# The first slots stage of a three-part language tower: from two passes of four sequences to one staggered sequence

## The chip, the cores and the metric

The kernel runs on one core of one Trainium2 chip. The metric is device time in microseconds (us), the median of several runs. The kernel is written by hand for the core's engines: TensorE (PE; its weight loads are shown as PEld), VectorE (DVE), ScalarE (ACT), GpSimd (POOL) and SyncE (SP, which issues the large DMAs). Each engine works off its own queue in order and waits on semaphores.

## What is computed

Eight sequences of 256 tokens with 192 features go through a token mixer, an attention layer and a two-level mixture of experts. The change lies at the start of the third part. Here is what matters of it, in the reference's words (G is the group of 64 tokens, g a token in it; e, s are 8 x 16 = 128 slots; the input h is first normalised per token over its 192 features):

```
xn = _l2norm(x) * scale * gamma_in
xg = xn.reshape(b, G, g, d)
phi = _l2norm(slots1) * scale
logits1 = jnp.einsum('bGgd,esd->bGges', xg, phi)
disp1 = jax.nn.softmax(logits1, axis=2)
comb1 = jax.nn.softmax(logits1.reshape(b, G, g, E1 * S1), -1)
slots = jnp.einsum('bGgd,bGges->bGesd', xg, disp1)
yn = _l2norm(slots) * scale * gamma2[None, None, :, None, :]
means = yn.reshape(b, G, E1, m, ns, d).mean(axis=4)
```

The stage leaves three things behind for the later ones: `yn`, the transposed `comb1` (`comb_t`) and the transposed `means` (`means_t`).

## The kernel before

The kernel is a chain of stages: `fold_weights` (folds weight products, and normalises and transposes the slot vectors into `phi_t`), `token_mixer`, `attention`, `first_slots`, `second_slots`, `second_dispatch`, `experts`, `combine`. A stage ends for all engines together, so what follows waits for the engine that ends last. All numbers are float32 in the stage that is changed. A float32 matmul appears in the trace as two MATMUL records, a transpose as one.

`first_slots` (L1181) treats the eight sequences in two passes of WIDE = 4. A sequence is 256 tokens, in TPS = 2 tiles of 128, or GPS = 4 groups of 64. Each pass goes through the same steps, and each step is done for all four sequences before the next one begins, in the queue of each engine:

- VectorE: token statistics (L1361, L1367); ScalarE turns variances into factors with a Ln and an Exp (`root`, L1289 and L1292); VectorE centres and scales (L1376) and multiplies by `gamma_in` (L1383), which gives `x`.
- TensorE transposes `x` in four pieces of 96 features by 128 tokens (L1234); ScalarE copies them out of PSUM (L1297).
- TensorE makes the logits in both orientations, contracting 96 + 96 features: slots by tokens (L1242) and tokens by slots (L1246).
- VectorE takes the maxima of both (L1388, L1391); ScalarE takes the exponentials with their sums (dispatch L1304, combine L1308).
- VectorE divides the combine weights (L1398, L1400). TensorE transposes dispatch (L1253) and combine (L1259). ScalarE copies dispatch into zero-padded tiles `disp`, 64 rows at a time (L1317), and VectorE keeps combine (L1406).
- TensorE makes the slots, each group as a contraction over 128 rows of which 64 are zeros (L1267). ScalarE squares and sums them one by one (L1333, each waiting for the one before). VectorE forms the variance (L1423, L1429), ScalarE takes its root (L1322, L1325), VectorE scales the slots (L1415).
- TensorE averages four slots at a time (L1274), ScalarE copies the result (L1341), TensorE transposes it (L1280), VectorE keeps it (L1438). ScalarE also copies the scaled slots into `yn_all` (L1344), which is the last instruction of the stage.

PSUM has eight banks; sequence `s` of a pass owns banks 2s and 2s + 1. GpSimd only clears the padding of `disp` (L1460, L1461). SyncE issues the loads of the next weights at the start of the stage (L1466, L1473, L1474). The next stage starts with VectorE's copy at L1596.

The order of ScalarE's queue at the end of a pass is typical of how the order is written out by hand:

```
for s in range(WIDE):
    act.wait_ge(S["slots_made"], at(i, s))
    for gr in range(GPS):
        ...
    if s:
        root_slots(s - 1)
root_slots(WIDE - 1)
```

## Time and profile before

| what | value |
|---|---|
| median of 3 runs | 716.32 us (715.44 to 719.78) |
| the profiled execution | 714.86 us |
| its span, first to last instruction | 713.1 us |
| lies around the span | 1.8 us |
| mean granted TensorE clock | 0.875 of full speed |
| `first_slots` | 349 to 421 us of the span |
| busy over the whole span | PE 81%, DVE 55%, ACT 43%, POOL 9% |

Full speed is 2.4 GHz, and the clock is either at that level (1.00) or at 1.2 GHz (0.50); a value between is a mix of both over a stretch. A busy time is the union of an engine's instructions. Instructions overlap in their engine, so a row's mean duration can be longer than the distance between two starts: for the cost of a queue the distance counts, for a handover the end.

### The profile page before, as it was taken

The numbers are of one execution on the slowest core, as the hardware profiler recorded it, in microseconds if no ns is written. First come the engines' busy times: TensorE is split into PE (matmuls) and PEld (weight loads), VectorE is DVE, ScalarE is ACT, GpSimd is POOL, SyncE is SP. The second block draws the span as 40 slices with busy tenths as digits, with TensorE's granted clock in tenths as the row PEclk, the third lists the DMA queues.
The fourth block names the chain that finished last, engine by engine and source line by source line (L and its number), as shares of the span: only waits on it lengthen the run. The fifth ranks groups of instructions, "written<-read, shape, count | busy, mean of one in ns | idle before, by whom it ended". The sixth has DMA issues, their size and how long they took to land. (4 is left out here: it accounts for less than half of the span.)

```text
span 713.1 us, 12372 instructions
## 1 busy us (share of the span) xinstructions
PE 580.8 (81%) x4294; PEld 473.8 (66%) x4294; DVE 390.7 (55%) x972; ACT 303.6 (43%) x859; POOL 64.9 (9%) x82
## 2 busy tenths in 40 slices
PE   6497996468888998887486968788889999999945
PEld 5486796255666665664374835577778999999934
DVE  2128646577999999964456344455653333333315
ACT  1223333143667666553177856555553222222211
...
DMA packets 19652, 58.19 MB, mean 82 GB/s; under 512 B 2627, under 2 KB 9397, under 8 KB 19478
## 3 DMA queue, kind: packets, MB, share of 16 engines
...
q8 instruction: 27, 0.44, 0.3%
q14 instruction: 19, 0.16, 0.1%
...
## 5 line engine op out<-in xcount | busy, mean ns | idle before, releaser
L1896 DVE SCALAR_TENSOR_TENSOR ex_act_t<-banks,b_sb,ex_gelu 128x128 f32<-128x128 f32 x128 | 36.0, 344 | 95.4 <-ACT ex_gelu L1879 95.4
L1879 ACT ACTIVATE ex_gelu<-banks,b_sb 128x128 f32<-128x128 f32 x128 | 36.6, 369 | 100.7 <-PE banks L1853 100.7
L1848 PE MATMUL banks<-slots_t,w 128*128 128x128 f32 x512 | 62.5, 275 | 1.1 <-PEq L1608 1.1
L1848 PEld LDWEIGHTS banks<-slots_t,w 128*128 128x128 f32 x512 | 61.2, 192 | 1.5 <-issue 1.3
L1074 DVE TENSOR_REDUCE att_max<-banks 128x4 f32<-128x1024 f32 x48 | 58.6, 1220 | 3.3 <-PE banks L736 2.4
L924 ACT ACTIVATE att_prob<-banks 128x1024 f32<-128x1024 f32 x48 | 49.1, 1023 | 17.2 <-PE banks L759 17.2
L1866 PE MATMUL banks<-w,ex_act_t 128*128 128x192 f32 x256 | 50.2, 339 | 0.2 <-DVE ex_act_t L1896 0.2
L1866 PEld LDWEIGHTS banks<-w,ex_act_t 128*128 128x128 f32 x256 | 40.7, 189 | 4.3 <-DVE ex_act_t L1896 0.5
L1853 PE MATMUL banks<-slots_t,w 64*128 64x128 f32 x512 | 37.2, 285 | 0.0
L736 PE MATMUL banks<-k_t,q_t 96*128 96x256 bf16 x192 | 31.9, 292 | 4.2 <-DVE att_max L1074 4.1
L774 PE MATMUL banks<-att_prob,val 128*32 128x256 f32 x384 | 29.2, 427 | 7.0 <-ACT att_prob L924 6.8
...
L759 PE MATMUL banks<-q_t,k_t 104*128 104x256 bf16 x192 | 31.0, 286 | 4.0 <-ACT att_prob L924 3.0
L1853 PEld LDWEIGHTS banks<-slots_t,w 64*128 64x128 f32 x512 | 31.1, 187 | 3.9
L709 PE MATMUL banks<-ident_b,att_stack 128*96 128x128 bf16 x384 | 28.3, 231 | 5.2 <-DVE att_stack L1041 2.4
L679 PE MATMUL banks<-qkv_t_sb,xt 96*128 96x384 f32 (+1 forms) x64 | 29.1, 591 | 3.3 <-ACT xt L870 3.3
L709 PEld LDWEIGHTS banks<-ident_b,att_stack 128*96 128x96 bf16 x384 | 26.2, 132 | 7.4 <-DVE q_t L1045 3.5
L899 ACT COPY k_t<-banks 96x1024 bf16<-96x1024 bf16 x24 | 24.1, 1006 | 15.3 <-PE banks L709 15.3
L1166 POOL TENSOR_TENSOR att_qk<-att_qk,qk_weight 128x192 f32<-128x192 f32 x16 | 9.2, 599 | 211.5 <-DVE att_qk L1009 211.5
L1529 PE MATMUL banks<-w_slot,ss_mean_k 96*128 96x384 f32 x64 | 23.9, 523 | 3.5 <-DVE ss_mean_k L1596 2.4
L736 PEld LDWEIGHTS banks<-k_t,q_t 96*128 96x128 bf16 x192 | 16.3, 103 | 13.4 <-DVE att_max L1074 8.4
L759 PEld LDWEIGHTS banks<-q_t,k_t 104*128 104x128 bf16 x192 | 18.2, 101 | 9.8 <-ACT att_prob L924 4.5
...
## 6 DMA issues: line engine op xcount, KB each, us to landing
...
```

Of the source, the lines that this page charges most:

```text
L679: last = nc.tensor.matmul(g.ps[banks[1 + t]][:, 0:2 * DIM], x_t[s][0:k, c, t * P:(t + 1) * P], g.t["qkv_t"][0:k, c, 0:2 * DIM], start=(c = ...
L709: last = nc.tensor.transpose(bank[0:KS, h * SEQ + t * P:h * SEQ + (t + 1) * P], stack[:, row, :, :].rearrange("p a b -> p (a b)"), ident_b ...
L736: last = nc.tensor.matmul(g.ps[hh][:, t * SEQ:(t + 1) * SEQ], q_t[s][0:KS, h, t * P:(t + 1) * P], k_t[s][0:KS, h, :], start=True, stop=True)
L759: last = nc.tensor.matmul(g.ps[2 + hh][:, m * SEQ:(m + 1) * SEQ], k_t[s][:, h, m * P:(m + 1) * P], q_t[s][:, h, :], start=True, stop=True)
L774: last = nc.tensor.matmul(bank[32 * j:32 * j + 32, (q % 2) * SEQ:(q % 2 + 1) * SEQ], val[s][:, m, QH * q + j, :], prob[j // 2][:, j % 2, m ...
L924: nc.scalar.activation(prob[u][:, :, :, :].rearrange("p a b n -> p (a b n)"), flat(2, 4), ACT.Exp).then_inc(S["exped"], 1)
L1074: nc.vector.tensor_reduce(neg_max[:, 2 * u:2 * u + 2, :].rearrange("p a b -> p (a b)"), flat(0, 2).rearrange("p (g n) -> p g n", n=SEQ), A ...
L1848: nc.tensor.matmul(bank[:, j * P:(j + 1) * P], g.w1[e][:, first + j * P:first + (j + 1) * P], x[:, 0, :], start=(j == 0), stop=False, skip ...
L1853: last = nc.tensor.matmul(bank[:, j * P:(j + 1) * P], g.w1[e][part, 2 * HID + j * P:2 * HID + (j + 1) * P], x[part, 1, :], start=False, st ...
L1866: last = nc.tensor.matmul(out_bank(n)[:, 0:DIM], act_t[n % 2][:, j * P:(j + 1) * P], g.w2[e][:, j, :], start=(j == 0), stop=(j == HB - 1))
L1879: nc.scalar.activation(gelu[n % 2][:, j * P:(j + 1) * P], gate_bank(n)[:, j * P:(j + 1) * P], ACT.Gelu_apprx_tanh, bias=g.t["b1"][:, n, HB ...
L1896: nc.vector.scalar_tensor_tensor(out=act_t[n % 2][:, j * P:(j + 1) * P], in0=value_bank(n)[:, j * P:(j + 1) * P], scalar=g.t["b1"][:, n, j ...
```

## The change

`first_slots` is written again:

- It is one sequence of 12 steps n, with no pass and no loop. In step n, TensorE's queue holds the logits of sequence n, the combine transposes of n - 2, the means' transposes of n - 3, the dispatch transposes of n - 1, the feature transposes of n + 1, the slots of n - 1 and the means of n - 2. The other queues follow the same pattern.
- PSUM banks are given to steps: bank 0 means, 1 and 2 logits, 3 (`TURN`) all three kinds of transposes of 128 columns, 4 to 7 slots in turn. Tiles have two to four buffers instead of one for each of four sequences.
- The 384 features of two token tiles are transposed as three full pieces of 128 instead of four of 96. Features are contracted as 128 + 64: a full-array matmul and one on 64 rows of the array, rows 0 to 63 for tile 0 and rows 64 to 127 for tile 1. `phi_t` gets three pieces; `fold_weights` for that makes two copies of the normalised slot vectors and three transposes.
- The slots are made from 64 rows per group on halves of the array, with no zero padding. A column of ones beside `x` gives the sum of the dispatch weights in PSUM, so that the dispatch exponentials keep no sum; VectorE copies these sums out (two small copies).
- GpSimd makes `x` (centre, scale, multiply by gamma) and divides the combine weights, instead of VectorE. VectorE copies dispatch, instead of ScalarE, in one instruction. The maxima of a sequence are two reductions over two banks each. The four squares of a sequence no longer wait for one another. VectorE writes the scaled slots straight into `yn_all`.

The core of the diff (the second part, from MEANS on, replaces the body of `first_slots`; its indentation is reduced):

```
-            for c in range(2):
-                last = nc.tensor.transpose(g.ps[6][0:HALF, c * P:(c + 1) * P],
-                                           slots_raw[:, c * HALF:(c + 1) * HALF], g.ident[:, :])
+            for c in range(3):
+                last = nc.tensor.transpose(g.ps[6][:, c * P:(c + 1) * P],
+                                           slots_two[:, c * P:(c + 1) * P], g.ident[:, :])
                     last.then_inc(slots_turned, 1)
...
-            nc.vector.tensor_scalar(slots_raw[:, :], slots_raw[:, :], slots_rn[:, :], ROOT, ALU.mult,
-                                    ALU.mult).then_inc(slots_normed, 1)
+            for c in range(2):
+                nc.vector.tensor_scalar(slots_two[:, c * DIM:(c + 1) * DIM], slots_raw[:, :], slots_rn[:, :],
+                                        ROOT, ALU.mult, ALU.mult).then_inc(slots_normed, 1)
...
-    nc.vector.tensor_copy(g.phi_t[:, :, :], g.ps[6][0:HALF, 0:2 * P].rearrange("p (c n) -> p c n", c=2)
+    nc.vector.tensor_copy(g.phi_t[:, :, :], g.ps[6][:, 0:3 * P].rearrange("p (c n) -> p c n", c=3)
...
+        MEANS, LOGITS, TURN = 0, (1, 2), 3
+        SLOTS = lambda n: (4 + 2 * (n % 2), 5 + 2 * (n % 2))
+        AND_ONE = lambda t: slice(t * (DIM + 1), (t + 1) * (DIM + 1))
...
+    def turn(n):
+        pe.wait_ge(S["weighted"], n + 1)
+        if n >= 2:
+            pe.wait_ge(S["disp_kept"], n - 1)
+        for c in range(3):
+            last = nc.tensor.transpose(g.ps[TURN][:, c * P:(c + 1) * P],
+                                       x[n % NX][:, 1 + c * P:1 + (c + 1) * P], g.ident[:, :])
+        last.then_inc(S["turned"], 1)
+
+    def logits(n):
+        pe.wait_ge(S["kept"], n + 1)
+        pe.wait_ge(S["disp_exped"], GPS * n)
+        pe.wait_ge(S["comb_exped"], TPS * n)
+        for part in range(2):
+            for to_slots in (True, False):
+                for t in range(TPS):
+                    rows, c = chunks(t)[part]
+                    of_x, of_phi = x_t[n % 2][rows, c, :], g.phi_t[rows, c, :]
+                    lhs, rhs = (of_phi, of_x) if to_slots else (of_x, of_phi)
+                    first = 0 if to_slots else P
+                    last = nc.tensor.matmul(g.ps[LOGITS[t]][:, first:first + P], lhs, rhs,
+                                            start=(part == 0 and to_slots), stop=(part == 1),
+                                            skip_group_check=True)
+        last.then_inc(S["logits"], 1)
+
+    def turn_comb(n):
+        pe.wait_ge(S["combined"], n + 1)
+        pe.wait_ge(S["kept"], min(n + 3, BATCH))
+        for t in range(TPS):
+            last = nc.tensor.transpose(g.ps[TURN][:, t * P:(t + 1) * P], comb[n % NC][:, t, :], g.ident[:, :])
+        last.then_inc(S["comb_turned"], 1)
+
+    def turn_disp(n):
+        pe.wait_ge(S["disp_exped"], GPS * (n + 1))
+        pe.wait_ge(S["kept"], min(n + 2, BATCH))
+        pe.wait_ge(S["comb_kept"], n)
+        for t in range(TPS):
+            last = nc.tensor.transpose(g.ps[TURN][:, t * P:(t + 1) * P],
+                                       disp_t[n % 2][:, t * P:(t + 1) * P], g.ident[:, :])
+        last.then_inc(S["disp_turned"], 1)
+
+    def make_slots(n):
+        pe.wait_ge(S["disp_kept"], n + 1)
+        pe.wait_ge(S["slots_normed"], GPS * (n - 1) if n else 0)
+        for t in range(TPS):
+            for half in range(2):
+                rows = slice(GROUP * half, GROUP * (half + 1))
+                last = nc.tensor.matmul(g.ps[SLOTS(n)[half]][:, AND_ONE(t)], disp[n % 2][rows, t, :],
+                                        x[n % NX][rows, AND_ONE(t)], start=True, stop=True)
+        last.then_inc(S["slots_made"], 1)
+
...
+    turn(0)
+    for n in range(BATCH + 4):
+        if n < BATCH:
+            logits(n)
+        if 0 <= n - 2 < BATCH:
+            turn_comb(n - 2)
+        if 0 <= n - 3 < BATCH:
+            turn_means(n - 3)
+        if 0 <= n - 1 < BATCH:
+            turn_disp(n - 1)
+        if n + 1 < BATCH:
+            turn(n + 1)
+        if 0 <= n - 1 < BATCH:
+            make_slots(n - 1)
+        if 0 <= n - 2 < BATCH:
+            make_means(n - 2)
...
+    def disp_exp(n):
+        act.wait_ge(S["maxed"], 2 * n + 2)
+        if n >= 2:
+            act.wait_ge(S["disp_turned"], n - 1)
+        for gr in range(GPS):
+            t, half = gr // 2, gr % 2
+            nc.scalar.activation(disp_t[n % 2][:, gr * GROUP:(gr + 1) * GROUP],
+                                 g.ps[LOGITS[t]][:, half * GROUP:(half + 1) * GROUP], ACT.Exp,
+                                 bias=neg_slot[:, n, t, half:half + 1]).then_inc(S["disp_exped"], 1)
+
+    def comb_exp(n):
+        if n >= NC:
+            act.wait_ge(S["comb_turned"], n - NC + 1)
+        for t in range(TPS):
+            nc.scalar.activation(comb[n % NC][:, t, :], g.ps[LOGITS[t]][:, P:2 * P], ACT.Exp,
+                                 bias=neg_tok[:, n, t:t + 1], accum_out=comb_sum[:, n, t:t + 1]
+                                 ).then_inc(S["comb_exped"], 1)
+
+    def squares(n):
+        act.wait_ge(S["slots_made"], n + 1)
+        act.wait_ge(S["squared"], GPS * n)
+        for gr in range(GPS):
+            nc.scalar.activation(square[:, gr, :], slots_of(n, gr), ACT.Square,
+                                 accum_out=slot_ss[:, n, gr:gr + 1]).then_inc(S["squared"], 1)
...
+    keep(0)
+    root(1)
+    for n in range(BATCH + 4):
+        if 0 <= n - 3 < BATCH:
+            keep_mean_rows(n - 3)
+        if 0 <= n - 2 < BATCH:
+            squares(n - 2)
+            root_slots(n - 2)
+        if n < BATCH:
+            disp_exp(n)
+        if n + 1 < BATCH:
+            keep(n + 1)
+        if n < BATCH:
+            comb_exp(n)
+        if n in (1, 3):
+            root(2 + n // 2)
...
+    def maxima(n):
+        dve.wait_ge(S["logits"], n + 1)
+        both = g.psum[:, LOGITS[0]:LOGITS[1] + 1, :]
+        nc.vector.tensor_reduce(neg_slot[:, n, :, :], both[:, :, 0:P].rearrange("p t (h n) -> p t h n", h=2),
+                                AX.X, ALU.max, negate=True).then_inc(S["maxed"], 1)
+        nc.vector.tensor_reduce(neg_tok[:, n, :], both[:, :, P:2 * P],
+                                AX.X, ALU.max, negate=True).then_inc(S["maxed"], 1)
+
+    def invert(n):
+        dve.wait_ge(S["comb_exped"], TPS * (n + 1))
+        nc.vector.reciprocal(comb_inv[:, n, :], comb_sum[:, n, :]).then_inc(S["inverted"], 1)
+
+    def keep_comb(n):
+        dve.wait_ge(S["comb_turned"], n + 1)
+        nc.vector.tensor_copy(g.comb_t[:, n * SEQ:(n + 1) * SEQ], g.ps[TURN][:, 0:SEQ]
+                              ).then_inc(S["comb_kept"], 1)
+
+    def keep_disp(n):
+        dve.wait_ge(S["disp_turned"], n + 1)
+        if n >= 2:
+            dve.wait_ge(S["slots_made"], n - 1)
+        nc.vector.tensor_copy(disp[n % 2][:, :, :], g.ps[TURN][:, 0:SEQ].rearrange("p (t n) -> p t n", t=TPS)
+                              ).then_inc(S["disp_kept"], 1)
+
+    def slot_variance(n):
+        dve.wait_ge(S["squared"], GPS * (n + 1))
+        for t in range(TPS):
+            col = 0 if t == 0 else 2 * (DIM + 1) - 1
+            a = SLOTS(n)[0]
+            nc.vector.tensor_copy(slot_sum[:, n, 2 * t:2 * t + 2], g.psum[:, a:a + 2, col]
+                                  ).then_inc(S["sums_kept"], 1)
+        dve.wait_ge(S["sums_kept"], 2 * (n + 1))
+        nc.vector.scalar_tensor_tensor(out=eps_part[:, n, :], in0=slot_sum[:, n, :], scalar=1e-6,
+                                       in1=slot_sum[:, n, :], op0=ALU.mult, op1=ALU.mult
+                                       ).then_inc(S["eps_made"], 1)
+        dve.wait_ge(S["eps_made"], n + 1)
+        nc.vector.tensor_tensor(slot_var[:, n, :], slot_ss[:, n, :], eps_part[:, n, :], ALU.add
+                                ).then_inc(S["var_made"], 1)
...
+    for n in range(4):
+        row_stats(n)
+    for n in range(BATCH + 4):
+        if n < BATCH:
+            maxima(n)
+        if 0 <= n - 2 < BATCH:
+            slot_variance(n - 2)
+            keep_comb(n - 2)
+        if 0 <= n - 1 < BATCH:
+            keep_disp(n - 1)
+        if 0 <= n - 2 < BATCH:
+            norm_slots(n - 2)
+        if 0 <= n - 3 < BATCH:
+            keep_means(n - 3)
+        if n + 4 < BATCH:
+            row_stats(n + 4)
+        if n < BATCH:
+            invert(n)
...
+    def make_x(n):
+        pool.wait_ge(S["rooted"], n // 2 + 1)
+        if n >= 2:
+            pool.wait_ge(S["weighted"], n - 1)
+        for t in range(TPS):
+            col = n * TPS + t
+            nc.gpsimd.tensor_scalar(centred[n % 2][:, t, :], g.h[:, col, :], mv[:, col, 0:1],
+                                    factor[:, col:col + 1], ALU.subtract, ALU.mult
+                                    ).then_inc(S["centred"], 1)
+        pool.wait_ge(S["centred"], TPS * (n + 1))
+        if n >= NX:
+            pool.wait_ge(S["slots_made"], n - NX + 1)
+        nc.gpsimd.tensor_tensor(x[n % NX][:, 1:1 + TPS * DIM].rearrange("p (t d) -> p t d", t=TPS),
+                                centred[n % 2][:, :, :],
+                                g.t["gamma_in"].unsqueeze(1).broadcast_to((P, TPS, DIM)), ALU.mult
+                                ).then_inc(S["weighted"], 1)
+
+    def scale_comb(n):
+        pool.wait_ge(S["inverted"], n + 1)
+        nc.gpsimd.tensor_tensor(comb[n % NC][:, :, :], comb[n % NC][:, :, :],
+                                comb_inv[:, n, :].unsqueeze(2).broadcast_to((P, TPS, P)), ALU.mult
+                                ).then_inc(S["combined"], 1)
+
+    for s in range(NX):
+        for col in (0, TPS * (DIM + 1) - 1):
+            nc.gpsimd.memset(x[s][:, col:col + 1], 1.0).then_inc(S["ones_set"], 1)
+    for n in range(3):
+        make_x(n)
+    for n in range(BATCH):
+        scale_comb(n)
+        if n + 3 < BATCH:
+            make_x(n + 3)
```

## Rows read from the trace of the kernel before

**Rows 1.** Windows view, the two passes (us; busy PE, PEld, DVE, ACT, POOL; PE clock; DMA).

```profile
348.00:388.00 40.00, 24.83 (x149) 20.00 (x149) 25.32 (x97) 23.06 (x109) 2.46 (x8) 0.76 0.42 148
...
388.00:424.00 36.00, 25.97 (x163) 20.76 (x162) 18.70 (x66) 26.87 (x112) 0.00 (x0) 0.83 0.00 1
```

**Rows 2.** Timeline, second pass (start us, length us, engine, line, operands, idle before).

```profile
390.27 2.05 PE L1234 MATMUL banks<-ident,fs_x 128*96 128x128 f32 x16 [1.29 <-DVE fs_x L1383]
...
390.95 2.04 ACT L1297 COPY fs_x_t<-banks 96x512 f32<-96x512 f32 x4 [0.30 <-PE banks L1234]
...
392.05 0.73 PEld L1242 LDWEIGHTS banks<-fs_x_t,phi_t 96*128 96x128 f32 x4
...
393.80 0.73 PEld L1242 LDWEIGHTS banks<-fs_x_t,phi_t 96*128 96x128 f32 x4
...
394.12 0.42 DVE L1388 TENSOR_REDUCE fs_neg_slot<-banks 128x4 f32<-128x256 f32 x1 [2.49 <-PE banks L1246]
...
394.96 0.31 ACT L1304 ACTIVATE fs_disp_t<-banks,fs_neg_slot 128x64 f32<-128x64 f32 x1 [1.98 <-DVE fs_neg_tok L1391]
...
401.68 0.49 ACT L1308 ACTIVATE fs_comb<-banks,fs_neg_tok 128x128 f32<-128x128 f32 x1
...
402.64 0.17 DVE L1398 RECIPROCAL fs_comb_inv<-fs_comb_sum 128x2 f32<-128x2 f32 x1 [0.90 <-ACT fs_comb L1308]
...
403.18 1.46 DVE L1406 COPY comb_t<-banks 128x256 f32<-128x256 f32 x4
...
409.83 0.20 ACT L1322 ACTIVATE fs_slot_log<-fs_slot_var 128x4 f32<-128x4 f32 x1
...
410.30 1.39 DVE L1415 SCALAR_TENSOR_TENSOR fs_yn<-banks,fs_slot_fac,gamma_sb 128x192 f32<-128x192 f32 x4
```

**Rows 3.** Timeline of TensorE in the experts stage, 560 to 568 us.

```profile
561.03 1.95 PE L1848 MATMUL banks<-slots_t,w 128*128 128x128 f32 x16
...
562.91 1.16 PE L1853 MATMUL banks<-slots_t,w 64*128 64x128 f32 x16
```

**Rows 4.** Groups of ScalarE by line and shape, whole kernel (count, busy us, mean ns, idle).

```profile
L1333 ACT ACTIVATE fs_square<-banks 128x192 f32<-128x192 f32 x32 | 10.5, 329 | 3.1 <-PE banks L1267 2.2
...
L893 ACT COPY val<-banks 128x384 f32<-128x384 f32 x8 | 3.8, 478 | 16.6 <-PE banks L688 16.6
```

**Rows 5.** Timeline of VectorE in the token mixer, a small operation that waited for the one before it.

```profile
64.80 0.16 DVE L513 TENSOR_TENSOR stat<-stat,mean_sq 128x4 f32<-128x4 f32 x1
```

**Rows 6.** Timeline, first pass.

```profile
349.04 2.17 DVE L1361 BATCH_NORM_STATS2 fs_bn<-h 128x6 f32<-128x192 f32 x8 [0.40 <-PEq L596]
...
355.55 3.65 PE L1234 MATMUL banks<-ident,fs_x 128*96 128x128 f32 x16 [7.50 <-DVE fs_x L1383]
```

**Rows 7.** Groups of GpSimd by line and shape, whole kernel.

```profile
L1166 POOL TENSOR_TENSOR att_qk<-att_qk,qk_weight 128x192 f32<-128x192 f32 x16 | 9.2, 599 | 211.5 <-DVE att_qk L1009 211.5
...
L342 POOL TENSOR_TENSOR placed<-h,pos_sb 128x384 f32<-128x384 f32 x4 | 4.0, 999 | 11.4 <-DVE y L567 11.4
```

**Rows 8.** Last stage: GpSimd's timeline, and line 1946 (ns: min/median/max).

```profile
695.29 6.85 POOL L1960 TENSOR_TENSOR co_rows<-yn_all,b_sb 128x768 f32<-128x768 f32 x3 [6.80 <-POOLq L1802]
...
L1946 DVE TENSOR_TENSOR co_rows<-yn_all,b_sb x4: 943/1488/2564, 695.3 to 705.0; 128x768 f32<-128x768 f32 x4
```

**Rows 9.** Windows view, two stretches of the attention stage.

```profile
148.00:156.00 8.00, 5.33 (x44) 4.76 (x45) 5.10 (x13) 4.30 (x8) 0.00 (x0) 0.60 0.00 0
...
324.00:332.00 8.00, 5.76 (x53) 3.63 (x54) 5.48 (x11) 3.55 (x4) 0.00 (x0) 1.00 0.01 2
```

**Rows 10.** Timeline, end of the stage.

```profile
417.04 0.87 PE L1274 MATMUL banks<-fs_yn,average 128*32 128x192 f32 x8 [0.43 <-DVE fs_yn L1415]
...
417.98 0.32 ACT L1341 COPY fs_mean_rows<-banks 128x192 f32<-128x192 f32 x1 [0.98 <-PE banks L1274]
...
418.19 3.03 ACT L1344 COPY yn_all<-fs_yn 128x768 f32<-128x768 f32 x4
...
418.61 1.73 DVE L1438 COPY means_t<-banks 96x128 f32<-96x128 f32 x8 [1.62 <-PE banks L1280]
```

333 lines of the change are left out of this document (97 added, 236 removed).

## The prediction

> **What bounds the kernel now.** I read the busy shares first: TensorE leads over the span, but the change touches one stage, so the next view is the windows of that stage. Between 348 and 424 us no engine is full [rows 1]: TensorE is busy for 24.8 of 40 us and then 26.0 of 36, ScalarE for 23.1 and 26.9, VectorE for 25.3 and 18.7, GpSimd for 2.5 in all. The stage is bound by handovers between engines that work in lock-step. The timeline shows them as idle times before the first instruction of a step: 1.29 us before the transposes, 2.49 before the first maximum, 1.98 before the first exponential [rows 2]. The stage ends with ScalarE's copies of `yn`, at 418.19 + 3.03 = 421.22 us [rows 10]; VectorE's last copy is out at 418.61 + 1.73 = 420.34. Everything before 349.04, VectorE's first instruction [rows 6], and after 421.22 stays as it is. So the question is when the new stage's last engine ends.
>
> **The new ring.** In the new code each step n has one chain that closes on itself, and I sum it, since the queues are in order. Logits(n) on TensorE wait for the exponentials of n - 1 (one buffer of logits banks). VectorE's queue then holds the maxima of n, the variance of n - 2 and the copy of combine n - 2. Only after that copy may TensorE transpose dispatch n - 1 into the same bank 3; VectorE copies that out; only then may TensorE transpose the features of n + 1, again into bank 3; ScalarE copies those, and behind that copy in its queue stand the combine exponentials of n, for which logits(n + 1) wait. The terms, at full clock:
>
> - Logits. The four matmuls over 128 rows are 8 records, the four on halves 8 more. The experts stage has both forms with 128 columns: 16 records in 1.95 us, 0.122 each, and 16 in 1.16, 0.073 each [rows 3]. So 0.98 + 0.58 = 1.56 us, against 393.80 - 392.05 = 1.75 now. The handover from the last matmul to the maximum is 394.12 - 393.80 = 0.32 [rows 2]. Together 1.88.
> - Maxima: two instructions of 256 elements in VectorE's queue, each about as far from the next as the copies of 256 at L1406, 1.46 / 4 = 0.365 [rows 2]: 0.73.
> - Variance: two small copies, then two operations that each wait. A small operation lasts 0.16 us [rows 5]; I take 0.20 per dependent step and 0.20 for the copies: 0.60. The squares are then ready: four at 0.33 [rows 4], some 0.35 apart, begin 0.7 us into the step and end at 2.1, before the maxima's 2.6.
> - Combine copy, 0.37 + 0.05 to hand over: 0.42.
> - Dispatch transposes. Four transposes took 390.95 - 390.27 = 0.68 us to ScalarE's start, at 2.05 / 16 = 0.13 each [rows 2]: two take 0.43, three 0.55. Here 0.43.
> - Dispatch copy: 0.42.
> - Feature transposes: 0.55.
> - ScalarE's copy of 384 columns: 0.48 [rows 4].
> - Combine exponentials to whoever waits: 402.64 - 401.68 = 0.96 [rows 2].
>
> Sum: 1.88 + 0.73 + 0.60 + 0.42 + 0.43 + 0.42 + 0.55 + 0.48 + 0.96 = 6.47 us a step, at most a few tenths more for instructions with two or three waits.
>
> What lies beside it: the dispatch exponentials end before the feature copy can start. TensorE's slots take 8 x 0.073 x 193/128 = 0.88 us on halves, behind the feature transposes and beside ScalarE's work. Scaling the slots takes VectorE 1.39 us [rows 2] after the dispatch copy, and the means follow at the end of the step, level with the exponentials. So the work taken from the padding, from the loops and from the `yn` copy is mostly off this chain. Of the moved work, only the `yn` copy shortens the end (0.88 us, 421.22 against 420.34).
>
> **Clock.** In the first pass, just after the stage begins, 16 transposes took 3.65 us against 2.05 in the second [rows 6, 2]: the clock was at 1.2 GHz, and the passes show 0.76 and 0.83 [rows 1]. At the lower level the chain grows by 1.56 (logits) and 5 x 0.10 = 0.50 (transposes), to 8.5 us. In the new stage TensorE has 1.56 + 9 x 0.13 + 0.88 + 0.87 (means, [rows 10]) = 4.5 us of work in 6.5, with one gap of about 1.7 us in each step (from the end of logits and old transposes to the dispatch transposes). Elsewhere such shares go either way: 5.33 of 8 us busy at 0.60, and 5.76 of 8 at 1.00 [rows 9]. I take the lower level for the first two steps and a quarter of the rest: 7.0 us a step.
>
> **GpSimd.** The trace of before shows no centring there. A two-input operation takes 0.60 us for 192 elements, 1.00 for 384 [rows 7]. For a one-input scaling of 192 I bound by half of the latter, 0.50, and by 0.60, and take 0.55. Making `x` is then 0.55 + 0.55 + 1.00 = 2.1 us, the combine division about 0.73 (between the two rows): 2.8 of 7 us, well hidden for all but the first sequence. It has another price. At L1946 a VectorE operation with two inputs in SBUF took 0.94 us at best and 2.56 while GpSimd did the same kind of work from 695.29 on [rows 8]: one held the other up. The variance has two such small operations on the chain. GpSimd starts the division when the inverses of the step before come, 0.1 to 0.7 us into a step, and its third instruction for `x` covers 2.0 to 3.6 us, over the variance at 2.8. It lasts for four steps (`x` is finished with sequence 7): between 0 and 0.7 us each, I take 1.6 us in all.
>
> The page "TensorEngine Tiling (Array Packing)" of the Trainium skill (Tiling Modes, Key Properties) says that changing the tiling mode drains TensorE. The experts rows bear it out little: the first matmul on a half starts at 562.91, before 561.03 + 1.95 = 562.98 [rows 3], and by that row a change costs nothing. By the rule the sum would be that of the third rival below.
>
> **The sum.** First logits: 349.04 + 1.7 (statistics of two sequences: four at 2.17 / 8, as many small aggregations at an estimated 0.1, two waits) + 0.57 (Ln and Exp, 410.30 - 409.83 and a handover) + 2.1 (`x`) + 0.9 (transposes at the lower clock) + 0.5 (copy) = 354.8; today the first `x` reaches TensorE at 355.55 [rows 6]. Step 0, all at the lower clock: 3.44 + 0.84 (both maxima, 394.96 - 394.12 [rows 2]) + 0.8 (dispatch exponentials) + 0.48 + 0.96 = 6.5. Step 1, no variance and no combine copy yet: 3.44 + 0.73 + 0.42 + 0.85 + 0.48 + 0.96 = 6.9. Steps 2 to 7: 6 x 7.0 = 42, and 1.6 for GpSimd. That is 411.8. The drain: means of 5 and their copy 0.65, squares of 6 1.4, variance 0.7, combine and dispatch of 6 and 7 0.42 + 0.43 + 0.37, scaling of 6 1.4, its means 0.94 (417.98 - 417.04) and copy 0.35 [rows 10], and then in line for sequence 7, whose squares stand behind that copy: squares 1.4, variance 0.7, root 0.47, scaling 1.39, means 0.94, copy 0.35, transposes 0.6, copies 2 x 0.22 + 0.06 = 0.5: 13.0 us. The end is at 424.8, against 421.2: 3.6 us later. `fold_weights` gets a third transpose, a second scaling and a wider copy, together under 1 us beside its waits for loads: 0, at most 1.
>
> The profiled execution took 714.86 us, which would become 718.5. The median of the runs is 1.46 above it, so the forecast is **720 us**.
>
> **Rivals.**
> 1. *The ring opens.* The chain's handovers are shorter than I read them or slip past one another, and the step is that of ScalarE's queue: 0.44 + 4 x 0.2 + 0.70 + 1.4 + 0.43 + 0.32, and 0.7 of waiting for the variance, 4.8 us. Then the stage ends 6 x 2.2 and the 1.6 earlier, 14.8, which is 11 below before: 705. For it: no engine has more than 5 us a step. Against it: three kinds of transposes share one bank and the order is fixed.
> 2. *The clock stays low.* The gap of 1.7 us keeps TensorE at 1.2 GHz; the place is logits and transposes in steps 2 to 7, the price 6 x 1.5 = 9 us less 1 for GpSimd, which is then past: 728. It decides, beyond 1%, once about half of these steps are at the lower level instead of a quarter. For it, the 0.60 at a busy share of two thirds; against it, the 1.00 beside it [rows 9].
> 3. *Each change between full array, halves and 32 columns empties TensorE.* Priced by the handover of 0.32, two or three changes on the chain, 8 steps: 5 to 8 us, 726.
> 4. *The stagger does not take hold.* Slower handovers with several waits each, 0.1 us at nine places in eight steps, 7 us: 727.
>
> **How the numbers follow.** Forecast 0.60 (its own range 714 to 725), ring opens 0.13, clock 0.13, mode changes 0.07, waits 0.07. About 1%, 7 us, is what a measurement of this kernel can tell from no change. Faster by more than that (below 709): 0.13. Slower (above 723.5): three rivals, mostly, 0.23, and 0.05 of the forecast's own spread, 0.28. Within: 0.59. The range must reach down toward the open ring and up to the low clock: 709 to 729.
>
> **What would show it.** Right: eight logits groups about 7 us apart, first at 355, last VectorE copy of the stage near 425; before logits(n + 1) TensorE waits for ScalarE's combine exponentials; before each dispatch transpose it waits for VectorE's combine copy; the second small variance operation is stretched in steps 2 to 5. Wrong: steps under 6 us, or TensorE waiting for GpSimd's `x`, or a granted clock near 0.5 throughout.

## The result, and the profile after

| | before | changed |
|---|---|---|
| median of 20 runs | 716.35 us (709.5 to 719.99) | 720.6 us (715.95 to 725.81) |
| profiled execution | 714.86 us, span 713.1, clock 0.875 | 717.03 us, span 715.3, clock 0.878 |
| first statistics of the stage to its last copy by VectorE or ScalarE | 349.04 to 421.22: 72.2 us | 344.32 to 422.08: 77.8 us |
| next stage's first copy | 421.6 | 422.46 |

The ratio is 1.007, with a 95% interval from 1.0038 to 1.0102: 0.4 to 1.0 per cent slower, within the 1% that the prediction took as its bound, and 0.6 us from the forecast. (Ratios leave out disturbed executions, so that they can differ from what two medians give, here 1.0059.)

The profiled executions differ by 2.2 us only because the changed kernel came to the stage 4.7 us earlier. But for one transpose and one scaling more in `fold_weights`, the code ahead of it does the same work in both. What differs is the clock between 28 and 330 us, 0.90 against 0.88. It isn't the change: in the variants below whose code ahead of the stage is that of the changed kernel, the stage began anywhere from 343.0 to 348.9 us. So I read the stage by itself: it is 5.6 us longer.

The profiled execution is also one of the faster of the changed kernel's twenty. Those at 717.6 us and below have a mean clock of 0.876 to 0.880, those above 722 us one of 0.865 to 0.875, so a typical execution spends more time at the lower level than the profiled one.

First the windows view (columns as in [rows 1]): the whole stage in the kernel before, then the whole stage and three stretches of it in the changed kernel.

```profile
349.04:421.60 72.56, 48.75 (x304) 39.60 (x304) 42.98 (x160) 49.94 (x220) 2.34 (x8) 0.80 0.23 82
```

```profile
344.32:422.46 78.14, 47.95 (x328) 32.26 (x328) 37.55 (x152) 33.86 (x168) 29.08 (x40) 0.74 0.22 77
376.00:408.00 32.00, 20.22 (x182) 13.92 (x182) 19.77 (x78) 18.31 (x92) 8.97 (x12) 1.00 0.00 1
408.00:424.00 16.00, 8.32 (x45) 4.03 (x39) 6.65 (x27) 4.30 (x23) 0.29 (x1) 0.50 0.01 2
424.00:428.00 4.00, 4.00 (x7) 2.02 (x6) 0.00 (x0) 0.00 (x0) 0.00 (x0) 0.50 0.00 0
```

ScalarE fell from 49.9 us to 33.9 and VectorE from 43.0 to 37.6, as the diff promises, and GpSimd rose from 2.3 to 29.1. Yet the stage is longer: no engine was its bound before and none is now. In the second fence, the second row is the steady part, at full clock, with TensorE busy 63%. The third is the drain, all at half clock; the fourth shows that the next stage's first matmuls begin at half clock too (the kernel before had 0.73 between 424 and 428 us).

The beginning of the stage, in the timeline:

```profile
346.74 2.01 POOL L1498 TENSOR_SCALAR fs_centred<-h,fs_mv,fs_factor 128x192 f32<-128x192 f32 x2 [2.12 <-ACT fs_factor L1334]
...
348.84 0.99 POOL L1504 TENSOR_TENSOR fs_x<-fs_centred,gamma_in_sb 128x384 f32<-128x384 f32 x1
...
349.98 0.88 PE L1244 MATMUL banks<-ident,fs_x 128*128 128x128 f32 x3 [6.58 <-POOL fs_x L1504]
...
351.42 1.22 PE L1259 MATMUL banks<-fs_x_t,phi_t 128*128 128x128 f32 x4 [0.57 <-ACT fs_x_t L1340]
```

The centring takes 1.00 us for a tile of 192 on GpSimd, as long as a two-input operation on 384; I had taken 0.55.

One step at full clock (sequence 4), TensorE and VectorE, with ScalarE's copy:

```profile
380.37 0.71 PE L1259 MATMUL banks<-fs_x_t,phi_t 128*128 128x128 f32 x4
...
380.92 0.61 PE L1259 MATMUL banks<-phi_t,fs_x_t 128*128 128x128 f32 x4
...
381.46 0.49 PE L1259 MATMUL banks<-fs_x_t,phi_t 64*128 64x128 f32 x4
...
381.79 0.39 PE L1259 MATMUL banks<-phi_t,fs_x_t 64*128 64x128 f32 x4
...
382.11 0.44 PE L1268 MATMUL banks<-ident,fs_comb 128*128 128x128 f32 x2
...
382.22 0.42 DVE L1412 TENSOR_REDUCE fs_neg_slot<-banks 128x4 f32<-128x256 f32 x1 [1.60 <-PE banks L1259]
...
383.15 0.16 DVE L1441 SCALAR_TENSOR_TENSOR fs_eps_part<-fs_slot_sum 128x4 f32<-128x4 f32 x1
383.34 0.16 DVE L1445 TENSOR_TENSOR fs_slot_var<-fs_slot_ss,fs_eps_part 128x4 f32<-128x4 f32 x1
...
383.42 0.42 DVE L1423 COPY comb_t<-banks 128x256 f32<-128x256 f32 x1
...
383.99 0.41 PE L1276 MATMUL banks<-ident,fs_disp_t 128*128 128x128 f32 x2 [1.22 <-DVE comb_t L1423]
384.44 0.42 DVE L1430 COPY fs_disp<-banks 128x256 f32<-128x256 f32 x1 [0.59 <-PE banks L1276]
384.78 1.38 DVE L1451 SCALAR_TENSOR_TENSOR yn_all<-banks,fs_slot_fac,gamma_sb 128x192 f32<-128x192 f32 x4
...
385.01 0.52 PE L1244 MATMUL banks<-ident,fs_x 128*128 128x128 f32 x3 [0.61 <-DVE fs_disp L1430]
...
385.56 0.48 ACT L1340 COPY fs_x_t<-banks 128x384 f32<-128x384 f32 x1 [0.76 <-PE banks L1244]
...
386.08 0.47 DVE L1458 COPY means_t<-banks 96x128 f32<-96x128 f32 x2
...
386.70 0.53 PE L1295 MATMUL banks<-yn_all,average 128*32 128x192 f32 x8 [0.32 <-DVE means_t L1458]
386.78 0.17 DVE L1419 RECIPROCAL fs_comb_inv<-fs_comb_sum 128x2 f32<-128x2 f32 x1 [0.23 <-ACT fs_comb L1357]
...
387.16 0.71 PE L1259 MATMUL banks<-fs_x_t,phi_t 128*128 128x128 f32 x4
```

Read it as a relay, each bracket naming the runner before. The chain of the prediction is all there: the combine copy at 383.42, for it the dispatch transposes at 383.99, their copy at 384.44, the feature transposes at 385.01, ScalarE's copy at 385.56. The last link is another one. The combine exponentials were done when VectorE inverted their sums at 386.78, but the logits of the next sequence start at 387.16. Ahead of them in TensorE's queue stand the means of sequence 2 (L1295), which waited for VectorE's copy of the means of sequence 1 (L1458), and that stands behind the scaling (L1451) in VectorE's queue. I had put that work "level with the exponentials"; it ends 0.3 us later. The step is 6.78 us, where the chain summed to 6.47.

Step 5 shows the collision with GpSimd:

```profile
389.71 0.99 POOL L1504 TENSOR_TENSOR fs_x<-fs_centred,gamma_in_sb 128x384 f32<-128x384 f32 x1
389.93 0.78 DVE L1441 SCALAR_TENSOR_TENSOR fs_eps_part<-fs_slot_sum 128x4 f32<-128x4 f32 x1
390.75 0.16 DVE L1445 TENSOR_TENSOR fs_slot_var<-fs_slot_ss,fs_eps_part 128x4 f32<-128x4 f32 x1
```

An operation on 4 elements a partition takes 0.78 us instead of 0.16, and ends with GpSimd's; the step takes 7.41. This happened once in eight sequences. The page "SBUF — State Buffer" of the Trainium skill (Who interferes with whom) says that a VectorE instruction with two inputs in SBUF contends with a GpSimd instruction that reads SBUF; these rows agree, with 0.78 us instead of 0.16.

### The profile page after: what moved, and what is told of

Same layout as the page of the kernel before. It is cut to its first block and busy times, and to the rows that moved or that the text cites. A ratio compares the mean times of both kernels' runs of the same rounds, so it can differ in the third digit from the quotient of the medians.

```text
span 715.3 us, 12386 instructions
## 1 busy us (share of the span) xinstructions
PE 576.8 (81%) x4319; PEld 464.8 (65%) x4319; DVE 385.1 (54%) x965; ACT 287.5 (40%) x807; POOL 91.6 (13%) x114
## 5 line engine op out<-in xcount | busy, mean ns | idle before, releaser
L738 PE MATMUL banks<-k_t,q_t 96*128 96x256 bf16 x192 | 30.1, 280 | 4.7 <-DVE att_max L1076 4.6
L776 PE MATMUL banks<-att_prob,val 128*32 128x256 f32 x384 | 27.4, 406 | 6.7 <-ACT att_prob L926 6.5
L681 PE MATMUL banks<-qkv_t_sb,xt 96*128 96x384 f32 (+1 forms) x64 | 29.1, 591 | 3.3 <-ACT xt L872 3.3
L761 PEld LDWEIGHTS banks<-q_t,k_t 104*128 104x128 bf16 x192 | 17.9, 100 | 10.2 <-ACT att_prob L926 4.5
L738 PEld LDWEIGHTS banks<-k_t,q_t 96*128 96x128 bf16 x192 | 15.6, 99 | 13.3 <-DVE att_max L1076 9.1
```

The source lines that it names most:

```text
L681: last = nc.tensor.matmul(g.ps[banks[1 + t]][:, 0:2 * DIM], x_t[s][0:k, c, t * P:(t + 1) * P], g.t["qkv_t"][0:k, c, 0:2 * DIM], start=(c = ...
L738: last = nc.tensor.matmul(g.ps[hh][:, t * SEQ:(t + 1) * SEQ], q_t[s][0:KS, h, t * P:(t + 1) * P], k_t[s][0:KS, h, :], start=True, stop=True)
L761: last = nc.tensor.matmul(g.ps[2 + hh][:, m * SEQ:(m + 1) * SEQ], k_t[s][:, h, m * P:(m + 1) * P], q_t[s][:, h, :], start=True, stop=True)
L776: last = nc.tensor.matmul(bank[32 * j:32 * j + 32, (q % 2) * SEQ:(q % 2 + 1) * SEQ], val[s][:, m, QH * q + j, :], prob[j // 2][:, j % 2, m ...
```

## The experiments

Each expectation names its own two theories; A is the one that I held when it was written. "Step" is the distance between the first maxima (L1412) of two sequences, and "the stage" goes from the first statistics to the next stage's first copy (78.1 us in the changed kernel). Ratios are to the kernel before on the same chip. Those of the changed kernel itself came from other batches, so differences of two or three thousandths are read from the traces and not from the ratios.

**1. The means' copy ahead of the dispatch copy.**

```
                 if 0 <= n - 2 < BATCH:
                     slot_variance(n - 2)
                     keep_comb(n - 2)
+                if 0 <= n - 3 < BATCH:
+                    keep_means(n - 3)
                 if 0 <= n - 1 < BATCH:
                     keep_disp(n - 1)
                 if 0 <= n - 2 < BATCH:
                     norm_slots(n - 2)
-                if 0 <= n - 3 < BATCH:
-                    keep_means(n - 3)
```

> One edit of the changed kernel: in VectorE's queue the copies of the means of n - 3 stand before the dispatch copy of n - 1 instead of behind the scaling of the slots of n - 2. Theory A (the ring is closed a second time: logits(n + 1) stand behind the means of n - 2 in TensorE's queue, and those wait for VectorE's scaling and, behind it, the copies of the means): the logits come 0.3 to 0.4 us earlier in each of six steps, step 6.4 to 6.5 us instead of 6.8, some 2 us in all, ratio to before about 1.004. Rival B (the ring as predicted, through the combine exponentials alone, is what holds): no change, step 6.8, ratio 1.007.

716.75 us, ratio 1.0031 [1.0006, 1.0055]. At full clock the step is 6.49 us: the second link is shown, and without it the chain of the prediction is right to 0.02. In the profile the stage is nevertheless 79.3 us. Two long steps follow one collision:

```profile
381.64 0.99 POOL L1504 TENSOR_TENSOR fs_x<-fs_centred,gamma_in_sb 128x384 f32<-128x384 f32 x1
381.70 0.95 DVE L1445 TENSOR_TENSOR fs_slot_var<-fs_slot_ss,fs_eps_part 128x4 f32<-128x4 f32 x1
...
383.13 0.66 PE L1276 MATMUL banks<-ident,fs_disp_t 128*128 128x128 f32 x2 [2.01 <-DVE comb_t L1423]
```

and its windows just around and after it:

```profile
376.00:384.00 8.00, 5.12 (x43) 3.31 (x42) 5.55 (x21) 5.04 (x26) 3.58 (x4) 0.92 0.00 0
384.00:392.00 8.00, 6.50 (x39) 4.56 (x39) 3.29 (x14) 3.06 (x16) 3.59 (x4) 0.65 0.01 2
392.00:400.00 8.00, 6.05 (x42) 4.05 (x43) 3.98 (x17) 4.14 (x22) 0.61 (x1) 0.79 0.00 0
```

TensorE idles 2.01 us, the clock falls, and the next steps take 9.77 and 7.85 us. So 0.8 us of lock came with 4.6 us more in two steps. That the gap brought the clock down is what the order suggests; it isn't shown by itself, and the changed kernel's gap of 1.85 us, after its own collision, was followed by a full clock.

**2. A bank of its own for the dispatch transposes** (96 + 96 features, the logits of both tiles in one bank; the orders unchanged).

```
-        MEANS, LOGITS, TURN = 0, (1, 2), 3
+        MEANS, LOGITS, TURN, TURN_DISP = 0, 1, 3, 2
...
             def turn_disp(n):
                 pe.wait_ge(S["disp_exped"], GPS * (n + 1))
-                pe.wait_ge(S["kept"], min(n + 2, BATCH))
-                pe.wait_ge(S["comb_kept"], n)
+                pe.wait_ge(S["disp_kept"], n)
```

> Features contracted as 96 + 96 so that the logits of both tiles fit in one PSUM bank (as in e4), and the bank that this frees goes to the dispatch transposes, which then no longer wait for VectorE's combine copy. Orders of the queues as in the changed kernel. Theory A (the shared bank serialises copy, transpose, copy, transpose): against e4 the dispatch transposes start right after the logits, the step shortens by 0.5 to 0.9 us, 3 to 5 us in all, until VectorE's scaling and the means behind it hold the logits. Rival B (the bank is not what orders the step; ScalarE's wait for the variance is): same step as e4 within 0.2 us.

716.54 us, 1.0038 [1.0005, 1.007]. The step at full clock is 6.34 us, against 7.02 for the same contraction on a shared bank (experiment 4): the shared bank, with the waits that it needs, costs 0.68 us a step. Against experiment 4 the stage is 4.8 us shorter in the profile (79.1 against 83.9), about seven such steps, and by the ratios the kernel gained 12 us. Against the changed kernel it gained about 2 by the ratios: steps of 9.23, 9.09 and 7.39 us stand in its profile, again at a lower clock, and the first two of them begin with a variance operation held for 0.84 us.

**3. The features `x` made by VectorE**, in GpSimd's order, with its operations.

```
+            dve.wait_ge(S["ones_set"], 2 * NX)
+            for n in range(3):
+                make_x(n)
             for n in range(BATCH + 4):
...
                     row_stats(n + 4)
+                if n + 3 < BATCH:
+                    make_x(n + 3)
```

> VectorE makes x as before the change (centre, scale, gamma), GpSimd only divides the combine weights. Theory A (GpSimd's three instructions of 1.0 us each delay the first logits, and once hold up a variance operation): first logits 1.5 to 2 us earlier after the stage begins, no stretched variance operation (0.6 us), the step unchanged at 6.8 as VectorE has the room; 2 to 2.5 us faster than the changed kernel, ratio to before 1.003 to 1.004. Rival B (VectorE is the scarce queue and GpSimd's help pays): 1.1 us more in each of the first five steps, 4 to 5 us slower than the changed kernel, ratio 1.013.

717.84 us, 1.0022 [0.9991, 1.0054]. No small operation is stretched any more. The first maximum comes 9.6 us after the stage's start instead of 10.38, a gain of 0.8 where I expected more: the first `x` waits for the statistics of four sequences in VectorE's queue. The step stays at 6.78, and the stage is 77.1 us. Two steps of 7.91 and 7.92 us stand before the steady ones, with this row in them:

```profile
376.00:384.00 8.00, 6.17 (x39) 4.02 (x38) 4.91 (x20) 3.66 (x18) 0.55 (x1) 0.71 0.00 0
```

So the clock can be low without any collision.

**4. The contraction back to 96 + 96, and nothing else** (two kernels of the same text, in two batches).

```
-                for c in range(3):
-                    last = nc.tensor.transpose(g.ps[TURN][:, c * P:(c + 1) * P],
-                                               x[n % NX][:, 1 + c * P:1 + (c + 1) * P], g.ident[:, :])
+                for c in range(2):
+                    for t in range(TPS):
+                        first = 1 + t * DIM + c * HALF
+                        last = nc.tensor.transpose(g.ps[TURN][0:HALF, c * SEQ + t * P:c * SEQ + (t + 1) * P],
+                                                   x[n % NX][:, first:first + HALF], g.ident[:, :])
...
-                            of_x, of_phi = x_t[n % 2][rows, c, :], g.phi_t[rows, c, :]
+                            of_x, of_phi = x_t[n % 2][:, part, t * P:(t + 1) * P], g.phi_t[:, part, :]
```

> Only the contraction is put back: features as 96 + 96, four transposes of 96 instead of three of 128, sixteen matmul records on 96 rows, a copy of 512 columns instead of 384; everything else as changed. The trace of the changed kernel shows its logits issued in 1.74 us, against 1.75 before the change and 1.56 in my sum. Theory A (array halves give nothing here, the third transpose and the narrower copy give a little): logits about 1.75 to 1.9 us, step 0.2 to 0.4 us longer, 2 to 3 us in all, ratio about 1.010. Rival B (the halves save their half of the array time): step 0.6 us longer or more, 5 us, ratio 1.014 or more.

> The kernel of e4 once more. Its steps at full clock were 7.0 us against 6.8, which makes 2 to 3 us, and its ratio to before was 1.020 where that makes 1.010. If steps at the lower clock level are what is over (two of its eight were 7.9 and 8.8 us), the ratio and the number of such steps in the new profile go together: with one such step less, 1.014 or lower. If something else costs, 1.020 again with steps as before.

732.22 us, 1.0204 [1.0147, 1.0261]; the second time 735.49, 1.020 [1.0149, 1.025]. The step at full clock is 7.02, 0.24 more. Over seven steps that is 1.7 us, and by the ratios the kernel lost some 10. In its profiled execution (725.37 us) the stage is 83.9 us, 5.8 more than in the changed kernel: the first two steps, mostly at half clock, are 0.6 and 1.0 longer, and two collisions fall in it instead of one (1.00 and 0.73 us), the second in a step of 8.84. Most of the other executions are longer still. The windows of one of the longest (738.08 us):

```profile
376.00:424.00 48.00, 41.79 (x207) 31.59 (x206) 18.09 (x73) 19.74 (x96) 12.01 (x14) 0.50 0.00 1
```

and of the shorter one (725.37 us):

```profile
376.00:424.00 48.00, 32.88 (x248) 23.14 (x248) 25.54 (x98) 24.23 (x122) 12.59 (x15) 0.86 0.00 1
```

In the first the clock doesn't rise again after 376 us, and every step from the fourth on takes 10.2 us. That is the far end, and the executions short of it go the same way: mean clocks of 0.846 to 0.853 at 731.16 to 733.55 us, against 0.870 to 0.874 at 723.77 to 725.37. So the halves came here with more than their 0.24 us a step: the changed kernel got to the full clock in the steady steps of its profile, and this one often doesn't. What decides that isn't settled, and that the 0.24 us brought it about is not shown by itself.

**5. Idle matmuls that keep TensorE busy**, in two kernels: `busy(k)` issues k matmuls of 128x120 on the identity, whose results nobody reads. At the entry, 13 before the first transposes and 5 in each of the first two steps:

```
+            busy(13)
             turn(0)
...
+                if n < 2:
+                    busy(5)
                 if 0 <= n - 1 < BATCH:
                     make_slots(n - 1)
```

> The changed kernel with idle matmuls (identity by 120 of its columns, into unused columns of bank 4, results never read): 13 of them before the first feature transposes, 5 more behind the feature transposes of steps 0 and 1. Nothing else changes. Theory A (TensorE's clock of 1.2 GHz in the first steps costs what the doubled records cost): granted clock at 1.00 by the first or second logits, the logits 1.7 us shorter in steps 0 and 1 and 1.1 in step 2, steps of 6.2, 6.6 and 7.9 us become about 4.5, 5.0 and 6.8; 4 to 5 us faster than the changed kernel, ratio to before 1.000 to 1.002. Rival B (the first steps are bound by GpSimd's x and by ScalarE, the clock is only a symptom): at most 1 us, ratio 1.006.

720.28 us, 1.0079 [1.0045, 1.0114]. The first maximum is 1.6 us earlier and the first two steps gain 1.4 and 1.1. Then the gain is lost: a step of 8.31, and, behind a variance operation held for 0.78 us, one of 9.73 while the clock is low (0.82 from 384 to 392, 0.71 to 400). Eleven of twelve runs lie between 718.8 and 721.6 us, so the kernel as a whole gained nothing; the start's gain, and where it was lost, are read from one profile.

In the drain, at the waits after the last logits:

```
+                if n == 10:
+                    busy(2)
                 if 0 <= n - 3 < BATCH:
                     turn_means(n - 3)
+                if n == 8:
+                    busy(6)
                 if 0 <= n - 1 < BATCH:
                     turn_disp(n - 1)
...
+                if n == 7:
+                    pe.wait_ge(S["comb_exped"], TPS * BATCH)
+                    busy(5)
+                if n == 9:
+                    busy(16)
                 if 0 <= n - 2 < BATCH:
                     make_means(n - 2)
+                if n == 10:
+                    busy(3)
```

> The changed kernel with the same kind of idle matmuls, in the logits bank after its last reader, at the end of the stage: 5 before the means of 5, 6 before the dispatch transposes of 7, 16 before the means of 7, 2 before and 3 behind the last transposes. The trace of the changed kernel has the clock at 0.50 from 408 to 428 us. Theory A: the clock stays at 1.00 there; means 0.35 us shorter twice, transposes 0.25 three times, and the first matmuls of the next stage in 2.8 us instead of 5.5: 2.5 to 4 us faster than the changed kernel, ratio to before 1.002 to 1.004. Rival B (the drain is bound by VectorE and ScalarE, and what the next stage's first matmuls lose they would lose anyway): under 1 us.

717.3 us, 1.0044 [1.001, 1.0077]. Its row for the drain and the next stage's start, and below it that of the changed kernel:

```profile
404.00:440.00 36.00, 29.61 (x202) 20.43 (x198) 15.14 (x53) 16.39 (x79) 1.23 (x2) 1.00 0.18 49
```

```profile
404.00:440.00 36.00, 25.06 (x108) 13.82 (x109) 14.19 (x48) 14.44 (x68) 0.61 (x1) 0.72 0.18 50
```

From the last maximum to the next stage it takes 18.5 us instead of 19.3, the next stage starts at full clock, and from there to the end the profile is 2.7 us shorter. By the ratios the kernel gained some 2 us, with intervals that overlap.

**6. The ring opened:** the banks of experiment 2, and new orders on three engines. On TensorE the dispatch transposes come right behind the logits, and combine transposes and means behind the slots, the means a step later. VectorE's queue becomes as follows; ScalarE roots the slots behind the combine exponentials, and copies the mean rows behind that.

```
                     maxima(n)
                 if 0 <= n - 2 < BATCH:
                     slot_variance(n - 2)
-                    keep_comb(n - 2)
                 if 0 <= n - 1 < BATCH:
                     keep_disp(n - 1)
-                if 0 <= n - 2 < BATCH:
-                    norm_slots(n - 2)
-                if 0 <= n - 3 < BATCH:
-                    keep_means(n - 3)
+                if 0 <= n - 4 < BATCH:
+                    keep_means(n - 4)
...
                     invert(n)
+                if 0 <= n - 2 < BATCH:
+                    keep_comb(n - 2)
+                    norm_slots(n - 2)
```

> The ring taken apart: features contracted as 96 + 96, the logits of both tiles in one bank, a bank of its own for the dispatch transposes, and the orders changed: on TensorE the means of n - 3 and their transposes a step later, combine transposes last; on ScalarE the root of the slots behind both exponentials; on VectorE the combine copy and the scaling last in the step. Theory A (the step is what its closed chain of handovers is, not what an engine has to do): logits 2.1, maxima 0.8, dispatch exponentials 0.8, copy 0.55, combine exponentials 0.9: steps of 5.2 us at full clock instead of 6.8, up to 10 us less in the stage, given back in part by a longer drain; ratio to before 0.993 to 0.998. Rival B (VectorE's queue or the clock is the next bound): steps of 6 us or more, ratio 1.000 or above.

710.3 us, 0.9933 [0.9896, 0.9969]: faster than both kernels. A step at full clock, from its timeline:

```profile
388.48 0.38 PE L1278 MATMUL banks<-ident,fs_disp_t 128*128 128x128 f32 x2
388.69 0.42 DVE L1415 TENSOR_REDUCE fs_neg_slot<-banks 128x4 f32<-128x256 f32 x1 [0.72 <-PE banks L1261]
388.71 0.60 PE L1247 MATMUL banks<-ident,fs_x 128*96 128x128 f32 x4
...
391.10 0.38 ACT L1359 ACTIVATE fs_comb<-banks,fs_neg_tok 128x128 f32<-128x128 f32 x1
...
392.05 0.71 PE L1261 MATMUL banks<-fs_x_t,phi_t 96*128 96x128 f32 x4
...
394.14 0.42 DVE L1415 TENSOR_REDUCE fs_neg_slot<-banks 128x4 f32<-128x256 f32 x1 [0.72 <-PE banks L1261]
```

Dispatch and feature transposes now run while VectorE still looks for maxima; the step is 5.45 us instead of 6.78, and 5.82 and 6.18 where GpSimd stretches an operation (0.52 and 0.88 us). (A third stretched one, of 0.83 us, stands in a step of 5.46.) The stage is 67.1 us. So the ring of the first rival can be opened, though to 5.45 us and not to the 4.8 of ScalarE's queue alone, and it took this reordering: in the changed kernel the rival's condition isn't met.

**7. The edits of experiments 1 and 3 together.**

> e1 and e3 together: the copies of the means before the dispatch copy, and x made by VectorE. Theory A (the two costs are separate: a second link of the ring, and GpSimd's slow start and its collision with the variance): their gains add, 0.4 and 0.5 per cent off the changed kernel, ratio to before 0.998 to 1.000, steps of 6.5 us at full clock and none stretched. Rival B (with x on it VectorE has no room left, so that the earlier copies only move the wait): no better than e3, ratio 1.002.

717.78 us (708.8 to 721.2), 1.0033 [0.9985, 1.0082]. The profiled execution has a stage of 72.3 us, steps of 6.49 but for one of 7.80 (at a clock of 0.82 from 380 to 388 us), no stretched operation, and a span of 710.8; the median shows nothing of it. Inconclusive.

**8. The opened ring, `x` of the first three sequences on VectorE, and idle matmuls at both ends.** Beside the edits of experiment 6:

```
+            busy(9)
             turn(0)
...
+                if n == 11:
+                    busy_late(3)
...
+                if n < 2:
+                    busy(4)
+                if n == 8:
+                    pe.wait_ge(S["comb_exped"], TPS * BATCH)
+                    busy_late(6)
                 if 0 <= n - 1 < BATCH:
                     make_slots(n - 1)
                 if 0 <= n - 2 < BATCH:
                     turn_comb(n - 2)
+                if n == 9:
+                    busy_late(6)
+                if n == 10:
+                    busy_late(2)
                 if 0 <= n - 3 < BATCH:
                     make_means(n - 3)
+            busy_late(3)
...
+            dve.wait_ge(S["ones_set"], 2 * NX)
+            for n in range(3):
+                make_x(n)
```

> e6 with x of the first three sequences made by VectorE and idle matmuls at both ends of the stage (9 before the first transposes, 4 in steps 0 and 1, 20 in the drain). Theory A (the costs are separate): against e6 the first logits come 1.6 us earlier, steps 0 and 1 lose 1.5 and 1.1 us, the drain and the next stage's first matmuls 1.3 to 2.5: 5 to 6 us less than e6, ratio to before 0.985 to 0.988. Rival B (what the clock gives at the start it takes back later in the stage, as in e5_warm_in, where two steps fell to the lower level): 1 to 3 us less than e6, ratio 0.989 to 0.992.

700.76 us (700.64 to 704.71), 0.9797 [0.977, 0.9824]: the best, 19.8 us under the changed kernel by the medians, and five of six runs within 0.3 us. That is more than theory A expected. Its rows for the steady part and for the drain with the next stage's start:

```profile
360.00:408.00 48.00, 38.49 (x335) 30.46 (x334) 31.93 (x125) 30.12 (x154) 16.26 (x19) 0.96 0.04 17
408.00:428.00 20.00, 18.30 (x81) 11.56 (x80) 7.39 (x15) 11.22 (x47) 0.00 (x0) 1.00 0.44 119
```

The first maximum comes at 8.4 us instead of 11.2 in experiment 6, the first step is 0.6 us shorter than there and the second the same, the stage takes 64.7, and the stage after it begins at full clock. Of the 10.1 us between the spans of the two profiles, 2.4 lie in the stage and 4.0 behind it. The other 3.7 lie ahead of it, where the two kernels are the same, so they are no gain of these edits that the runs show. Against the profile of the changed kernel, whose stage begins within 0.1 us of this one's, the stage is 13.4 us shorter and what follows 3.4.

**9. Experiment 3 with idle matmuls at the entry**, as in experiment 5, with 9 instead of 13 at first.

> e3 (x on VectorE, so that no variance operation is held up by GpSimd) with the idle matmuls of e5_warm_in at the start (9, and 5 in steps 0 and 1). In e5_warm_in the start gained 4 us, and right behind a variance operation held up by GpSimd the clock fell, for two long steps. Theory A (the held-up operation is what makes TensorE's idle time in the step long enough for the clock to fall): all steps from 2 on at 6.8 us and 1.00, 4 us faster than e3, ratio to before 0.997. Rival B (the clock falls on its own in this ring, with a third of each step idle, wherever its turns come): steps of 8 to 10 us remain, ratio 1.001 or more.

715.36 us, 0.9989 [0.9969, 1.0009]. The stage is 73.7 us, with the start's gain kept: first maximum at 8.0, first steps 4.77 and 5.5. But steps of 7.95 and 7.91 follow, at a clock of 0.71 between 368 and 376, and here no small operation was stretched. So the clock can fall without a collision, which the reading of experiment 1 alone doesn't cover. Over the profiles the picture is mixed: a step at a lower clock begins with a collision of 0.7 us or more in experiments 1, 2 (twice), 4 and 8 (one of two in each) and 5 (entry); collisions of that size went by at full clock in the changed kernel, in the drain's kernel of experiment 5 and in experiment 6; and the clock fell without one in experiments 3, 7, 9 and 10. A collision is at most one of several ways there.

**10. The edits of experiments 6 and 3 together:** the opened ring with all of `x` on VectorE.

> e6 with all of x made by VectorE. In e6 the step is 5.45 us, and three steps were lengthened by GpSimd holding up a variance operation, by 0.4 to 0.7 us each; VectorE has about 4.7 us of work in an early step, 1.15 more with x. Theory A (VectorE becomes the bound of the opened ring while it also makes statistics and x): steps 1 to 4 of about 6 us, later ones 5.45, the first logits 1.6 us earlier: within 1 us of e6, ratio 0.992 to 0.994. Rival B (there is room enough): 3 us faster than e6, ratio 0.989.

714.46 us, 0.9964 [0.994, 0.9989]: 4 us above experiment 6 by the medians, 3 thousandths by the ratios, whose intervals overlap. The steps are again 5.45 at full clock, so VectorE did not become the bound; but there are two of 7.15 and 8.49 us. The rows before and in the second of them:

```profile
376.00:384.00 8.00, 6.39 (x57) 5.02 (x56) 6.00 (x24) 4.74 (x25) 0.89 (x2) 1.00 0.00 0
384.00:392.00 8.00, 6.10 (x33) 4.70 (x33) 5.05 (x20) 3.96 (x20) 0.61 (x1) 0.62 0.01 2
```

So taking `x` off GpSimd, collisions and all, gained nothing in the opened ring, and neither theory had the low clock in it.

## Why the prediction came out right

The time was right within 0.1%, and the mechanism too (the drain's row in the table starts at 406.5, where the combine exponentials of sequence 7 end): the stage is a ring of handovers, and with 16.1 us of work less on ScalarE and 5.4 less on VectorE it is no shorter. The terms were less good than the sum:

| | predicted | measured |
|---|---|---|
| start to first logits | 5.8 | 351.42 - 344.32 = 7.1 |
| steps 0 and 1 | 13.4 | 364.52 - 351.42 = 13.1 |
| steps 2 to 7, with GpSimd's 1.6 | 43.6 | 42.0 |
| drain | 13.0 | 15.6 |
| sum | 75.8 | 77.8 |

- **First logits.** `x` takes 3.2 us from the factors to the transposes, 2.1 predicted: "half of a two-input operation on 384" was too low for a centring with two scalars by pointer. It takes 1.00 for each of the two tiles, as much as a whole operation on 384.
- **Logits.** 382.11 - 380.37 = 1.74 us, not 1.56, and so as long as the 1.75 before. The rows of [rows 3] came from runs of 16 alike; here groups of four alternate (whether that is the cause is not shown), and a record over 128 rows takes (381.46 - 380.37) / 8 = 0.136 us, one on a half 0.08. Against 96 + 96 in the same staggered code the halves save 0.15 us of logits (1.89 there in experiment 6) and 0.1 in ScalarE's copy (0.48 against 0.58), which is about the 0.24 of experiment 4.
- **The chain.** Right but for the link through the means (0.3 us a step). Its other terms err both ways and nearly cancel. In the step shown it takes 6.41 us from the first logits to the inversion at 386.78, against 6.47: a VectorE copy with its handover to TensorE takes 0.57 instead of 0.42, twice, and the maxima, the variance, ScalarE's copy and the exponentials take some 0.1 us less each. Experiment 1, without that link, has 6.49.
- **Clock.** I took half clock for two steps and a quarter of the rest. The profile shows 0.50 up to 364, 0.62 and about 0.8 up to 376, and full clock for steps 4 to 7. The price of a step at the lower level was far too low: 2.0 us predicted, 3.2 measured (10.2 against 7.02, experiment 4, for 96 + 96, in the profile of 738.08 us). The chain was stretched in its logits and transposes only. At the lower level the slots and means close it: in the changed kernel's step 2 the slots run from 370.98 and the means until 373.44, and the next logits start at 373.36, 1.1 us after ScalarE's last exponential. The second rival was thus cheaper on paper than on the chip, and for the contraction of 96 it is what happens in that profile.
- **GpSimd.** The mechanism was right and it was rarer: 0.6 us in all, not 1.6, since the overlap must hit one of two operations of 0.16 us; it hit the first of them in one step, not the second in four. What I had left out is that a lower clock may follow, as in experiments 1 and 2, which is not shown to come of it.
- **Step 7** is short (5.13 us), because there are no features left to transpose. I had counted a full one.
- **Drain.** 2.6 us too little. The squares of sequence 6 start 2.06 us into it, where I had 0.65: with the short step 7, VectorE's scaling of sequence 5 and the means' copy behind it are left over, and the means wait for that copy. Twice more the link that I had missed returns, for 0.9 us in all:

```profile
417.66 1.39 DVE L1451 SCALAR_TENSOR_TENSOR yn_all<-banks,fs_slot_fac,gamma_sb 128x192 f32<-128x192 f32 x4 [0.18 <-ACT fs_slot_fac L1373]
418.97 0.47 DVE L1458 COPY means_t<-banks 96x128 f32<-96x128 f32 x2
...
419.59 0.87 PE L1295 MATMUL banks<-yn_all,average 128*32 128x192 f32 x8 [3.63 <-DVE means_t L1458]
```

  The half clock is the smaller part: my term for the means came from a row that was itself at 0.87 us [rows 10], and experiment 5 in the drain, at full clock, is 0.7 us shorter.
- **What follows the stage.** Put at nothing in the sum: from its end to the end of the kernel it takes 1.3 us more than before, with the next stage's first matmuls at half clock for longer. Experiment 5 in the drain shows that this can be had back.
- **Mode changes** (third rival): no pause. The first matmul on a half starts at 381.46, before 380.92 + 0.61 = 381.53, and the groups of four follow one another at 0.55, 0.54, 0.33 and 0.32 us, with nothing added at the change to the halves or at the change back. The rule of the page "TensorEngine Tiling (Array Packing)" of the Trainium skill (Tiling Modes, Key Properties), that TensorE drains at such a change, cost nothing that these rows show.

In the profile the stage and what follows cost 6.9 us, in the medians 4.3 us; the interval of the ratio, 2.7 to 7.3 us, holds both. The sum had 3.6 us for the two. The forecast of 720 was helped by terms that erred both ways, and by luck: the medians lie nearer to each other than the profiles' stages do.
